# A gated attention and feed-forward block on one core: the order of the first batch's preparation is changed

## The chip, the core and the metric

The kernel runs on one core of a Trainium2 chip. The metric is the device time of one execution in microseconds (us), given as the median of the runs of the same program. The engines are PE (matrix products), DVE (the vector engine), ACT (the scalar engine), POOL (GpSimd) and SP, which only issues transfers. Each works through its own list of instructions in the order in which they are written, and they meet only at semaphores.

## The reference

For x of shape (8, 512, 256), in float32 (normalisation over the last axis, weights 256 x 256 and 1024 x 256):

```
xn = layernorm(x)
q, k, v = gelu(xn @ W1n + b1n) @ W2n + b2n            # n = q, k, v
scores  = tril(q @ k^T / sqrt(256 * 512))             # no softmax
s       = layernorm(scores @ v) * ln_w + ln_b
Wq1, Wq2 = clip(round(W / (mean(abs(W)) + eps)), -1, 1)   # ternary W1 and W2 of the FFN
g       = silu(relu(xn @ Wq1^T + b1) @ Wq2^T + b2)
out     = x + s * g
```

## The kernel before

Every engine's program is written out by hand. A batch (one of the eight 512 x 256 slices of x) goes through the stages below on PE; batch 0 is written apart (`first=True`), batches 1 to 6 run in a loop, batch 7 is apart again. Most operands are split in a rounded part ("hi") and the rest ("lo"), and a product is the sum of three products of such parts (`split_product`, line 843; all its matmuls show as L849 in the profile). Each hi part is made by ACT or POOL and each lo part mostly by DVE.

PE's stages in a batch are: layer one (six 128 x 512 products in the order `ORDER`, each followed on ACT by two GELU passes, L443 and L444, and on DVE by one `g_lo`, L653), K (two products that make z), V, F1 (eight products with the ternary W1), the key sum D, the scores S, Y0, Y1 (FFN output with the ternary W2), the weighted sums O, and Y2. Eight PSUM banks are handed round; `claim` waits until the bank's former content has been read.

Batch 0 has work that no other batch has:

- **Transposes.** DVE normalises the first batch (`x_normalise0`, L576), PE transposes it (`transpose_x`, L833), ACT and DVE make hi and lo parts (`xT_hi` at L427, `xT_lo` at L633).
- **Folding.** q and k are only needed as a product, so W2q and W2k are multiplied into one matrix: `fold_weights(0)` and `(1)` on PE, `fold_hi` on ACT (L431), `fold_lo` on DVE (L622, L624). The bias terms are `fold_z_bias` (twice) and `fold_d_bias`, each two matmuls of one column; DVE copies their results at L676 and L677.
- **Quantising.** ACT and DVE sum the absolute values of W1 (`abs_sum1`, L402; L637) and of W2 (`abs_sum2`, L408), PE adds over partitions (`sum_partitions`), DVE makes the thresholds (`thresholds`, L589, L591) and then the ternary weights: `quantise1(0)` and `(1)` for the two halves of W1 (L596 a comparison, L598 a comparison with subtraction), `quantise2` for five of the eight blocks of W2. POOL does the other three blocks (`quantise_rest`: L310, L311, L314). It begins when DVE has finished `quantise2` (semaphore `w2_quantized`). Y0 on PE waits for all of W2 (`w2_rest_quantized`) and for all eight `r_lo` parts of DVE (L743).
- **Parts of the key sum.** `e32` is made by DVE (L667, L678); in batch 0 POOL makes its parts (L339, L341).
- **Second batch's input.** `x_statistics(1)` on DVE (L554 to L547), then POOL normalises two tiles (`xn1_tile`, L303) and DVE two.

`v_shift_of` on ACT (L413) sums the rows of W2v, which POOL then needs for the centred W2v. PE begins with `WARM_UP` matmuls on a tile of ones (L840), whose result nobody reads.

SP issues the loads in one order: half of x[0], W1k, W2q, W1q, W2k, W2v, x[1], W1v, W1 of the FFN in two parts, W2 of the FFN. The biases (`cols`) and the other half of x[0] come from ACT's queue.

Of the kernel before, what the change touches and what calls it, by code (L numbers as in the profile page):

```python
# [27 lines left out]
AT_X0, AT_X1 = ((2, 3), (4, 6)), 30  # L28
# [6 lines left out]
WARM_UP = 17  # L35


def gated_block(nc, x, x_t, x_norm_rows, w_qkv, w1t, w2t, cols, rows, out):
# [13 lines left out]
    with ctx:  # L52
# [141 lines left out]
        def _(sp):  # L194
# [6 lines left out]
            sp.dma_start(x_all[:, 0, 0:2], x[0, 0:2 * P].rearrange("(t p) c -> p t c", p=P)).then_inc(x0_loaded[0], 16)  # L201
            load_square(1)
            sp.dma_start(w2q_raw[:, :, 0:C], w_qkv[3].rearrange("(k p) c -> p k c", p=P)).then_inc(qkv_loaded[3], 16)
            load_square(0)
            load_square(4)
# [49 lines left out]
        def _(pool):  # L255
# [72 lines left out]
            def batch(i, first=False, second_last=False, last=False):  # L328
                if first:
                    pool.wait_ge(x_rstd_made, 1)  # L330
                    pool.wait_ge(xT_summed, 2 * CK)
                    pool.wait_ge(w1_quantized, 1)
                    xn1_tile(0)
                    xn1_tile(1)
                    pool.wait_ge(v_shift_made, CK + 1)
                    nc.gpsimd.tensor_scalar(row[:, ROW_B2V], row[:, ROW_B2V], v_shift[:, CK:CK + 1], None,
                                            ALU.add).then_inc(v_centred, 1)
                    pool.wait_ge(e_made, 1)
                    nc.gpsimd.tensor_copy(e["hi"][:], e32[:]).then_inc(e_hi_made, 1)  # L339
                    pool.wait_ge(e_hi_made, 1)  # L340
                    nc.gpsimd.tensor_tensor(e["lo"][:], e32[:], e["hi"][:].bitcast(FP32),  # L341
                                            ALU.subtract).then_inc(e_split, 1)
                    pool.wait_ge(w2_quantized, 1)
                    quantise_rest()
                elif not last:
                    pool.wait_ge(xT_loaded, 16 * i)
                    pool.wait_ge(x_norm_loaded, 16 * i)
                    for k in range(CK):
                        xT_centre(k)
                        xT_scale(i + 1, k)  # L350
# [35 lines left out]
        def _(act):  # L386
# [48 lines left out]
            for k in range(CK):  # L435
                v_shift_of(k, raw_qkv[:, 5, k])

            def batch(i, first=False, last=False):
                for p, m in enumerate(ORDER):
                    act.wait_ge(l1_summed, 6 * i + p + 1)  # L440
                    b1 = col[:, COL_B1 + m:COL_B1 + m + 1]
                    pre = bank[(AT_L1 + p) % BANKS]
                    nc.scalar.activation(g["hi"][:, m], pre[:], ACT.Gelu, bias=b1)  # L443
                    nc.scalar.activation(pre[:], pre[:], ACT.Gelu, bias=b1).then_inc(l1_whole, 1)  # L444
                    if first and p < CK:
                        fold_hi(p)
                    if first and p == 0:
                        abs_sum1()
# [73 lines left out]
        def _(dve):  # L522
# [117 lines left out]
            def batch(i, first=False, second_last=False, last=False):  # L640
# [23 lines left out]
                if first:  # L664
                    fold_lo(0)
                    dve.wait_ge(fold_read, CK)
# [5 lines left out]
                if first:  # L672
                    fold_lo(1)
                    dve.wait_ge(fold_read, 2 * CK)
                    dve.wait_ge(biases_folded, 1)
                    nc.vector.tensor_copy(z_bias[:], FOLD_Z)  # L676
                    nc.vector.tensor_copy(d_const[:], FOLD_D).then_inc(bias_read, 1)  # L677
# [3 lines left out]
                if not first:  # L681
                    finish(i - 1, 2, 2, 2)
                if first:
                    thresholds(0)
                    dve.wait_ge(thr_made, 2)
                    quantise1(0)
                g_lo(2)
                g_lo(3)
                g_lo(4)
                g_lo(5)  # L690
                if first:
                    dve.wait_ge(w1_quantized, 1)
                    quantise1(1)
                    dve.wait_ge(w1_quantized, 2)
# [15 lines left out]
                if first:  # L710
                    thresholds(1)
# [106 lines left out]
        def _(pe):  # L818
# [41 lines left out]
            def fold_z_bias(n):  # L860

                split_product(FOLD_Z[:, n:n + 1], [(w2qT[:, k, n * P:(n + 1) * P], b2k[:, k:k + 1])
                                                   for k in range(CK)])
# [19 lines left out]
            def batch(i, first=False, last=False):  # L883

                pe.wait_ge(xT_hi_made, 2 * i + CK + 2)
                for p, m in enumerate(ORDER):
                    if first and p == 1:
                        pe.wait_ge(qkv_loaded[4], 16)
                        pe.wait_ge(b2q_beside, 1)
                    if first and p == 1:  # L890
                        fold_weights(0)
                    if first and p == 2:
                        fold_weights(1)
# [9 lines left out]
                    if first and p == 3:  # L903
# [80 lines left out]

            transpose_x(xn_made, AT_X0[0], (0, 1))
            pe.wait_ge(qkv_loaded[3], 16)
            pe.wait_ge(cols_loaded, 16)
            fold_z_bias(0)
            transpose_x(xn_made, AT_X0[1], (2, 3))
            fold_z_bias(1)  # L990
            fold_d_bias()
# [36 lines left out]
```

## Time and profile before

| | us |
|---|---|
| median of 3 runs | 307.86 |
| lowest and highest | 307.18, 310.16 |
| the profiled execution | 307.08 |
| its span, first to last instruction | 305.3 |

| engine | busy, us | share of the span |
|---|---|---|
| PE (matmul) | 299.3 | 98% |
| PE (weight load) | 268.6 | 88% |
| DVE | 247.9 | 81% |
| ACT | 222.2 | 73% |
| POOL | 132.8 | 43% |

The granted clock of PE is 1.000 over the span. The time outside the span is 307.08 - 305.3 = 1.8 us. In the timeline a row merges instructions of one kind that follow each other: start, time from the start of the first to the end of the last, engine, line, what is written and read, how many, and in brackets how long the engine stood idle before and what released it. The ends of matmuls and of pipelined vector instructions reach over the start of the next one, so a stage's length is best read from start to start.

### The profile page before, as it was taken

The numbers are of one execution on the slowest core, as the hardware profiler recorded it, in microseconds if no ns is written. First come the engines' busy times: TensorE is split into PE (matmuls) and PEld (weight loads), VectorE is DVE, ScalarE is ACT, GpSimd is POOL, SyncE is SP. The second block draws the span as 40 slices with busy tenths as digits, with TensorE's granted clock in tenths as the row PEclk, the third lists the DMA queues.
The fourth block names the chain that finished last, engine by engine and source line by source line (L and its number), as shares of the span: only waits on it lengthen the run. The fifth ranks groups of instructions, "written<-read, shape, count | busy, mean of one in ns | idle before, by whom it ended". The sixth has DMA issues, their size and how long they took to land.

```text
span 305.3 us, 5721 instructions
## 1 busy us (share of the span) xinstructions
PE 299.3 (98%) x1852; PEld 268.6 (88%) x1852; DVE 247.9 (81%) x548; ACT 222.2 (73%) x428; POOL 132.8 (43%) x104
## 2 busy tenths in 40 slices
PE   8999999999999999999999999999999999999994
PEld 8878899889988899888997889888998889988893
DVE  4989898957999589975999669995799858696686
ACT  3696958966785957949489577868679594895862
POOL 3954835076060942439151670608515291404100
PEclk9999999999999999999999999999999999999999
DMA  7960044500006000240005100060001500020001
GB/s 236 374 217 1 1 140 137 182 26 0 3 2 206 0 0 0 65 141 0 0 0 145 62 0 0 1 204 2 0 0 39 168 0 0 0 71 2 0 2 69
DMA packets 15228, 19.06 MB, mean 62 GB/s; under 512 B 1776, under 2 KB 12528, under 8 KB 15216
## 3 DMA queue, kind: packets, MB, share of 16 engines
q1 hardware_dynamic: 14656, 18.51, 18.6%
q10 hardware_dynamic: 560, 0.40, 0.4%
q8 instruction: 6, 0.10, 0.2%
q14 instruction: 6, 0.05, 0.1%
HBM read 14.69 MB, written 4.22 MB: 62 GB/s over the span
## 4 chain that ended last, share of the span: by engine, by line
PE 87%; DVE 6%; DMA 3%; SPq 1%; ACT 1%; issue 1%; POOL 0%; DVEq 0%
PE bank L849 86%; DMA x_all<-in_w1t 3%; DVE g L653 1%; SPq L199 1%; DVE gw L767 1%; DVE gw L645 0%; DVE w1q L598 0%; DVE x_all L647 0%; PE bank L957 0%; DVE e L756 0%; PE bank L958 0%; ACT r_lo L402 0%; DVE s_lo L738 0%; DVE gw L796 0%; PE bank L833 0%
## 5 line engine op out<-in xcount | busy, mean ns | idle before, releaser
L743 DVE TENSOR_TENSOR r_lo<-bank,r_hi 128x512 fp32r<-128x512 f32 x64 | 44.0, 691 | 34.7 <-ACT bank L465 34.6
L464 ACT ACTIVATE r_hi<-bank,col 128x512 fp32r<-128x512 f32 x64 | 47.0, 734 | 24.3 <-PE bank L849 24.3
L361 POOL TENSOR_TENSOR o_rstd<-o_var,neg_half 128x2 f32<-128x2 f32 x16 | 11.2, 699 | 82.8 <-ACT o_var L495 82.8
L465 ACT ACTIVATE bank<-bank,col 128x512 f32<-128x512 f32 x64 | 45.4, 710 | 0.0
L320 POOL TENSOR_TENSOR y<-y,xn 128x512 f32<-128x512 f32 x12 | 19.8, 1648 | 55.6 <-DMA y<-in_x_t 55.6
L849 PE MATMUL bank<-xT_lo,w1q 128*128 128x512 f32 x128 | 39.5, 390 | 0.0
L849 PE MATMUL bank<-xT_hi,w1q 128*128 128x512 f32 x128 | 39.5, 390 | 0.0
L443 ACT ACTIVATE g<-bank,col 128x512 fp32r<-128x512 f32 x48 | 34.2, 713 | 1.3 <-PE bank L849 1.1
L849 PE MATMUL bank<-w2q,r_lo 128*128 128x256 f32 x256 | 34.6, 278 | 0.0
L849 PE MATMUL bank<-w2q,r_hi 128*128 128x256 f32 x256 | 34.3, 276 | 0.0
L444 ACT ACTIVATE bank<-bank,col 128x512 f32<-128x512 f32 x48 | 33.0, 688 | 0.0
L479 ACT CAST s_hi<-s 128x512 fp32r<-128x512 f32 (+3 forms) x32 | 14.8, 461 | 23.2 <-DVE s L731 17.8
L849 PEld LDWEIGHTS bank<-w2q,r_lo 128*128 128x128 f32 x256 | 31.6, 188 | 0.0
L849 PEld LDWEIGHTS bank<-w2q,r_hi 128*128 128x128 f32 x256 | 31.4, 188 | 0.0
L653 DVE TENSOR_TENSOR g<-bank,g 128x512 fp32r<-128x512 f32 x48 | 30.7, 681 | 0.0
L849 PE MATMUL bank<-xT_hi,w_hi 128*128 128x512 f32 x96 | 30.3, 396 | 0.0
L849 PE MATMUL bank<-xT_hi,w_lo 128*128 128x512 f32 x96 | 29.7, 390 | 0.0
L849 PE MATMUL bank<-xT_lo,w_hi 128*128 128x512 f32 x96 | 29.6, 389 | 0.0
L849 PEld LDWEIGHTS bank<-xT_hi,w1q 128*128 128x128 f32 x128 | 24.0, 188 | 5.1
L849 PEld LDWEIGHTS bank<-xT_lo,w1q 128*128 128x128 f32 x128 | 23.5, 188 | 4.4
L849 PE MATMUL bank<-g,z_hi 128*128 128x512 f32 (+2 forms) x96 | 22.0, 337 | 0.0
L849 PEld LDWEIGHTS bank<-xT_hi,w_lo 128*128 128x128 f32 x96 | 18.0, 188 | 3.8
(143 smaller groups left out, 684.8 us busy)
## 6 DMA issues: line engine op xcount, KB each, us to landing
out<-x_all SPq DMA_DIRECT2D x15, 256.0 KB, 3.1
x_all<-in_x SPq DMA_DIRECT2D x7, 512.0 KB, 3.6
xn<-x_norm_rows SPq DMA_DIRECT2D x6, 512.0 KB, 4.0
y<-in_x_t SPq DMA_DIRECT2D x6, 512.0 KB, 4.7
x_all<-in_w1t SPq DMA_DIRECT2D x2, 512.0 KB, 7.6
x_all<-in_w2t SPq DMA_DIRECT2D x1, 1024.0 KB, 10.2
row<-in_rows SPq DMA_DIRECT2D x1, 512.0 KB, 4.7
x_all<-in_x SPq DMA_DIRECT2D x1, 256.0 KB, 3.2
```

Source lines behind the costliest of these rows:

```text
L199: sp.dma_start(raw_qkv[:, n], w_qkv[n].rearrange("(k p) c -> p k c", p=P)).then_inc(qkv_loaded[n], 16)
L320: nc.gpsimd.tensor_tensor(half, half, x_mean_all, ALU.subtract).then_inc(xT_centred, 1)
L361: nc.gpsimd.tensor_tensor(o_rstd[:, half], o_var[:, half], neg_half[:, half], ALU.pow).then_inc(o_rstd_made, 1)
L443: nc.scalar.activation(g["hi"][:, m], pre[:], ACT.Gelu, bias=b1)
L444: nc.scalar.activation(pre[:], pre[:], ACT.Gelu, bias=b1).then_inc(l1_whole, 1)
L464: nc.scalar.activation(r["hi"][:, f], pre[:], ACT.Relu, bias=b1)
L465: nc.scalar.activation(pre[:], pre[:], ACT.Relu, bias=b1).then_inc(f1_whole, 1)
L479: nc.scalar.copy(s["hi"][:, at], s32[:, at]).then_inc(s_hi_made, 1)
L653: nc.vector.tensor_tensor(g["lo"][:, m], bank[(AT_L1 + p) % BANKS][:], g["hi"][:, m].bitcast(FP32), ALU.subtract).then_inc(g_split, 1)
L743: nc.vector.tensor_tensor(r["lo"][:, f], bank[(AT_F1 + f) % BANKS][:], r["hi"][:, f].bitcast(FP32), ALU.subtract).then_inc(r_split, 1)
L767: nc.vector.scalar_tensor_tensor(gw[:, t], bank[(AT_O + t) % BANKS][:, 0:C], o_rstd[:, t:t + 1], row[:, ROW_LNW], ALU.mult, ALU.mult).then ...
L849: last = nc.tensor.matmul(dst, a, b, start=(n == 0), stop=(n == len(pairs) - 1))
```

## The change

Batches 1 to 7 keep their code. In batch 0 and ahead of it:

- SP loads W2q and W2k directly after the first half of x[0]; W1k becomes the fourth transfer of its queue (it was the second) and W1q the fifth (it was the fourth).
- PE does 14 warm-up matmuls where it did 17. Then come the bias folds and `fold_weights(0)` ahead of the transposes, and `fold_weights(1)` behind them; layer one has no fold in it. The sum over partitions for W1 stands after the fifth product of layer one and no longer after the fourth. One bank of the transposes is another (`AT_X0`).
- ACT does `fold_hi(0)` ahead of the first GELU, `fold_hi(1)` after the first pair, `abs_sum1` after the second pair.
- DVE does `fold_lo(0)` and the two bias copies ahead of `x_statistics(1)`, `fold_lo(1)` behind it; all six `g_lo` come ahead of `quantise1(0)`; `thresholds(0)` stands after the fourth `g_lo`, `thresholds(1)` after `quantise1(1)`.
- POOL makes the parts of the key sum and shifts the bias row ahead of `xn1_tile`, behind a wait for all six `g_lo`.

```diff
-AT_X0, AT_X1 = ((2, 3), (4, 6)), 30
+AT_X0, AT_X1 = ((2, 3), (4, 1)), 30
-WARM_UP = 17
+WARM_UP = 14
@@ SP
             sp.dma_start(x_all[:, 0, 0:2], x[0, 0:2 * P].rearrange("(t p) c -> p t c", p=P)).then_inc(x0_loaded[0], 16)
+            sp.dma_start(w2q_raw[:, :, 0:C], w_qkv[3].rearrange("(k p) c -> p k c", p=P)).then_inc(qkv_loaded[3], 16)
+            load_square(4)
             load_square(1)
-            sp.dma_start(w2q_raw[:, :, 0:C], w_qkv[3].rearrange("(k p) c -> p k c", p=P)).then_inc(qkv_loaded[3], 16)
             load_square(0)
-            load_square(4)
@@ POOL, batch 0
                 if first:
+                    pool.wait_ge(g_split, 6)
+                    pool.wait_ge(e_made, 1)
+                    nc.gpsimd.tensor_copy(e["hi"][:], e32[:]).then_inc(e_hi_made, 1)
...
                     pool.wait_ge(w1_quantized, 1)
                     xn1_tile(0)
                     xn1_tile(1)
...
                     pool.wait_ge(w2_quantized, 1)
                     quantise_rest()
@@ ACT
             for k in range(CK):
                 v_shift_of(k, raw_qkv[:, 5, k])
+            fold_hi(0)
...
-                    if first and p < CK:
-                        fold_hi(p)
                     if first and p == 0:
+                        fold_hi(1)
+                    if first and p == 1:
                         abs_sum1()
@@ DVE
+            fold_lo(0)
+            dve.wait_ge(biases_folded, CK + 1)
+            nc.vector.tensor_copy(z_bias[:], FOLD_Z)
+            nc.vector.tensor_copy(d_const[:], FOLD_D).then_inc(bias_read, 1)
             x_statistics(1, second=True)
+            fold_lo(1)
...
+                g_lo(2)
+                g_lo(3)
                 if first:
                     thresholds(0)
+                g_lo(4)
+                g_lo(5)
+                if first:
                     dve.wait_ge(thr_made, 2)
                     quantise1(0)
-                g_lo(2)
-                g_lo(3)
-                g_lo(4)
-                g_lo(5)
-                if first:
                     dve.wait_ge(w1_quantized, 1)
                     quantise1(1)
+                    thresholds(1)
@@ PE, layer one of batch 0
-                    if first and p == 1:
-                        fold_weights(0)
-                    if first and p == 2:
-                        fold_weights(1)
...
-                    if first and p == 3:
+                    if first and p == 4:
                         pe.wait_ge(abs1_summed[0], 1)
@@ PE, ahead of batch 0
-            transpose_x(xn_made, AT_X0[0], (0, 1))
-            pe.wait_ge(qkv_loaded[3], 16)
-            pe.wait_ge(cols_loaded, 16)
-            fold_z_bias(0)
-            transpose_x(xn_made, AT_X0[1], (2, 3))
-            fold_z_bias(1)
-            fold_d_bias()
+            pe.wait_ge(cols_loaded, 16)
+            fold_d_bias()
+            pe.wait_ge(qkv_loaded[3], 16)
+            fold_z_bias(0)
+            fold_z_bias(1)
+            pe.wait_ge(qkv_loaded[4], 16)
+            pe.wait_ge(b2q_beside, 1)
+            fold_weights(0)
+            transpose_x(xn_made, AT_X0[0], (0, 1))
+            transpose_x(xn_made, AT_X0[1], (2, 3))
+            fold_weights(1)
```

PE, from the bias folds or transposes to the end of the first product of layer one, before the change (`bank<-w2q_raw,raw_qkv` is `fold_weights`, `bank<-ident,xn` a transpose, the products of one column are the bias folds):

```order
L849 MATMUL bank<-col,w2q_raw 128x1 x2
L849 MATMUL bank<-col 128x1 x2
L849 MATMUL bank<-xT_hi,w_hi 128x512 [waits w_split,xT_hi_made]
L849 MATMUL bank<-xT_hi,w_hi 128x512
L849 MATMUL bank<-xT_hi,w_lo 128x512 x2
L849 MATMUL bank<-xT_lo,w_hi 128x512 [waits xT_split]
L849 MATMUL bank<-xT_lo,w_hi 128x512
L849 MATMUL bank<-w2q_raw,raw_qkv 128x257 [waits b2q_beside,qkv_loaded4]
L849 MATMUL bank<-w2q_raw,raw_qkv 128x257
L849 MATMUL bank<-xT_hi,w_hi 128x512 x2
```

The same place in the changed kernel, from the last warm-up matmuls on:

```order
L842 MATMUL bank<-ones 128x128 x13
L851 MATMUL bank<-col 128x1 [waits cols_loaded,consts_made]
L851 MATMUL bank<-col 128x1
L851 MATMUL bank<-col,w2q_raw 128x1 [waits qkv_loaded3]
L851 MATMUL bank<-col,w2q_raw 128x1 x3
L851 MATMUL bank<-w2q_raw,raw_qkv 128x257 [waits b2q_beside,qkv_loaded4]
L851 MATMUL bank<-w2q_raw,raw_qkv 128x257
L835 MATMUL bank<-ident,xn 128x128 [waits xn_made]
```

The folds stood inside layer one and behind the transposes; now three bias folds and the first weight fold stand ahead of the transposes.

DVE, from the lo parts of the transposed input to the first product's `g_lo`, before:

```order
L633 TENSOR_TENSOR xT_lo<-bank,xT_hi 128x256 [waits xT_hi_made] x4
L554 BN_STATS x_stats<-x_all 128x6 [waits x_loaded]
L554 BN_STATS x_stats<-x_all 128x6 x3
L544 BN_AGGR x_norm<-x_stats 128x2 [waits x1_stats_made]
L544 BN_AGGR x_norm<-x_stats 128x2 x3
L547 TENSOR_SCALAR x_var<-x_norm 128x4 [waits x1_stats_made]
L637 TENSOR_REDUCE abs_sum<-x_all 128x1 [waits raw1_loaded0]
L622 TENSOR_TENSOR w_lo<-bank,w_hi 128x256 [waits fold_hi_made,l1_whole]
L624 COPY d_weight<-bank 128x1
L667 TENSOR_SCALAR e<-bank,d_weight 128x512 [waits fold_read]
L653 TENSOR_TENSOR g<-bank,g 128x512 [waits l1_whole]
```

and now:

```order
L635 TENSOR_TENSOR xT_lo<-bank,xT_hi 128x256 [waits xT_hi_made] x4
L624 TENSOR_TENSOR w_lo<-bank,w_hi 128x256 [waits fold_hi_made]
L626 COPY d_weight<-bank 128x1
L639 COPY z_bias<-bank 128x2 [waits biases_folded]
L640 COPY d_const<-bank 128x1
L556 BN_STATS x_stats<-x_all 128x6 [waits x_loaded]
L556 BN_STATS x_stats<-x_all 128x6 x3
L546 BN_AGGR x_norm<-x_stats 128x2 [waits x1_stats_made]
```

The first `fold_lo` (L624 of the changed kernel), which waits for `fold_hi(0)` on ACT, now stands ahead of the statistics of the second batch.

POOL, in batch 0, as a difference (`L310` is the start of `quantise_rest`):

```order
 L299 TENSOR_TENSOR w2v_lo<-raw_qkv,w2v_hi 128x512 [waits w2v_hi_made]
-L303 TENSOR_SCALAR xn<-x_all,x_norm 128x256 [waits xT_summed,w1_quantized,x_rstd_made,rows_loaded]
+L332 CAST e_hi<-e 128x512 [waits e_made,g_split,rows_loaded]
+L334 TENSOR_TENSOR e_lo<-e,e_hi 128x512 [waits e_hi_made]
+L337 TENSOR_SCALAR row<-row,small 128x256 [waits v_shift_made]
+L303 TENSOR_SCALAR xn<-x_all,x_norm 128x256 [waits w1_quantized,xT_summed,x_rstd_made]
 L303 TENSOR_SCALAR xn<-x_all,x_norm 128x256
```

The two tiles of the second batch move behind the parts of the key sum; `quantise_rest` keeps its place and its wait.

## Rows read from the trace of the kernel before

**Rows 1.** The page: the span, and its part 4, the chain that ended last.

```profile
span 305.3 us, 5721 instructions
...
PE 87%; DVE 6%; DMA 3%; SPq 1%; ACT 1%; issue 1%; POOL 0%; DVEq 0%
```

**Rows 2.** The timeline of PE: start, length, engine, line, operation, count, idle before.

```profile
6.90 0.67 PE L833 MATMUL bank<-ident,xn 128*128 128x128 f32 x4
...
8.40 0.51 PE L849 MATMUL bank<-col,w2q_raw 128*128 128x1 f32 x4
8.77 0.59 PE L849 MATMUL bank<-col 128*128 128x1 f32 x4
9.21 0.70 PE L849 MATMUL bank<-xT_hi,w_hi 128*128 128x512 f32 x2
...
10.70 1.03 PE L849 MATMUL bank<-w2q_raw,raw_qkv 128*128 128x257 f32 x4
...
16.95 0.71 PE L849 MATMUL bank<-xT_hi,w_hi 128*128 128x512 f32 x2
...
19.80 0.62 PE L849 MATMUL bank<-g,w_hi 128*128 128x512 f32 x2
...
23.00 0.74 PE L849 MATMUL bank<-w2v_hi,g 128*128 128x256 f32 x4 [0.32 <-DVE g L653]
...
37.46 1.09 PE L849 MATMUL bank<-w2q,r_lo 128*128 128x256 f32 x8
```

**Rows 3.** Timeline of POOL: key-sum parts and its share of quantising W2.

```profile
25.75 1.29 POOL L341 TENSOR_TENSOR e_lo<-e,e_hi 128x512 fp32r<-128x512 f32 x1
30.63 2.22 POOL L310 TENSOR_SCALAR gw<-x_all,neg_thr 128x768 f32<-128x768 f32 x1 [3.59 <-DVE w2q L598]
...
35.20 1.85 POOL L314 TENSOR_TENSOR w2q<-w2q,gw 128x768 fp32r<-128x768 f32 x1
```

**Rows 4.** Timeline of DVE between 10 and 31 us.

```profile
10.28 1.41 DVE L554 BATCH_NORM_STATS2 x_stats<-x_all 128x6 f32<-128x256 f32 x4 [0.27 <-DMA x_all<-in_x]
...
16.30 0.42 DVE L622 TENSOR_TENSOR w_lo<-bank,w_hi 128x256 fp32r<-128x256 f32 x1 [1.01 <-ACT w_hi L431]
...
18.47 0.76 DVE L596 TENSOR_SCALAR s<-x_all,neg_thr 128x1024 f32<-128x1024 f32 x1
...
20.46 2.48 DVE L653 TENSOR_TENSOR g<-bank,g 128x512 fp32r<-128x512 f32 x4
22.86 0.88 DVE L596 TENSOR_SCALAR s<-x_all,neg_thr 128x1024 f32<-128x1024 f32 x1
...
25.23 1.41 DVE L699 SCALAR_TENSOR_TENSOR z_lo<-bank,z_bias,z_hi 128x512 fp32r<-128x512 f32 x2
...
30.56 0.69 DVE L743 TENSOR_TENSOR r_lo<-bank,r_hi 128x512 fp32r<-128x512 f32 x1
```

**Rows 5.** Warm-up matmuls (L840) by half microseconds: window, PE busy (instructions touched).

```profile
4.50:5.00 0.50, 0.50 (x4) 0.50 (x4) 1.00 0.87 284
...
5.50:6.00 0.50, 0.50 (x7) 0.50 (x7) 1.00 0.86 299
```

**Rows 6.** Timeline of SP, and DMA issues with us to landing (last column).

```profile
2.31 0.47 SPq L199 DMA_DIRECT2D raw_qkv<-in_W1q  x1
...
raw_qkv<-in_W1q SPq DMA_DIRECT2D x1, 256.0 KB, 4.9
```

**Rows 7.** Timeline of ACT ahead of and in layer one.

```profile
8.49 0.65 ACT L427 CAST xT_hi<-bank 128x256 fp32r<-128x256 f32 x2 [0.35 <-PE bank L833]
9.03 0.43 ACT L413 ACTIVATE o_square<-raw_qkv 128x256 f32<-128x256 f32 x1
...
10.90 0.69 ACT L443 ACTIVATE g<-bank,col 128x512 fp32r<-128x512 f32 x1 [0.95 <-PE bank L849]
...
12.05 0.39 ACT L431 CAST w_hi<-bank 128x256 fp32r<-128x256 f32 x1
...
13.59 1.06 ACT L402 ACTIVATE r_lo<-x_all 128x1024 fp32r<-128x1024 f32 x1 [1.15 <-DMA x_all<-in_w1t]
```

More of the change, by code:

```diff
@@ L329, in batch @@
                 if first:
+                    pool.wait_ge(g_split, 6)
+                    pool.wait_ge(e_made, 1)
+                    nc.gpsimd.tensor_copy(e["hi"][:], e32[:]).then_inc(e_hi_made, 1)
+                    pool.wait_ge(e_hi_made, 1)
+                    nc.gpsimd.tensor_tensor(e["lo"][:], e32[:], e["hi"][:].bitcast(FP32),
+                                            ALU.subtract).then_inc(e_split, 1)
+                    pool.wait_ge(v_shift_made, CK + 1)
+                    nc.gpsimd.tensor_scalar(row[:, ROW_B2V], row[:, ROW_B2V], v_shift[:, CK:CK + 1], None,
+                                            ALU.add).then_inc(v_centred, 1)
                     pool.wait_ge(x_rstd_made, 1)
@@ L334, in batch @@
                     xn1_tile(1)
[L335 to L342, printed above, removed]
                     pool.wait_ge(w2_quantized, 1)
@@ L664, in batch @@
                 if first:
-                    fold_lo(0)
                     dve.wait_ge(fold_read, CK)
@@ L672, in batch @@
                 if first:
-                    fold_lo(1)
                     dve.wait_ge(fold_read, 2 * CK)
-                    dve.wait_ge(biases_folded, 1)
-                    nc.vector.tensor_copy(z_bias[:], FOLD_Z)
-                    nc.vector.tensor_copy(d_const[:], FOLD_D).then_inc(bias_read, 1)
                 nc.vector.scalar_tensor_tensor(e32[:], bank[(AT_L1 + 1) % BANKS][:], d_weight[:, 1:2], e32[:],
@@ L682, in batch @@
                     finish(i - 1, 2, 2, 2)
+                g_lo(2)
+                g_lo(3)
                 if first:
                     thresholds(0)
-                    dve.wait_ge(thr_made, 2)
-                    quantise1(0)
-                g_lo(2)
-                g_lo(3)
                 g_lo(4)
@@ L691, in batch @@
                 if first:
+                    dve.wait_ge(thr_made, 2)
+                    quantise1(0)
                     dve.wait_ge(w1_quantized, 1)
                     quantise1(1)
+                    thresholds(1)
                     dve.wait_ge(w1_quantized, 2)
@@ L710, in batch @@
                 if first:
-                    thresholds(1)
                     dve.wait_ge(e_split, 1)
@@ L862, in fold_z_bias @@
                 split_product(FOLD_Z[:, n:n + 1], [(w2qT[:, k, n * P:(n + 1) * P], b2k[:, k:k + 1])
-                                                   for k in range(CK)])
+                                                   for k in range(CK)]).then_inc(biases_folded, 1)
             def fold_d_bias():
@@ L886, in batch @@
                 for p, m in enumerate(ORDER):
-                    if first and p == 1:
-                        pe.wait_ge(qkv_loaded[4], 16)
-                        pe.wait_ge(b2q_beside, 1)
-                    if first and p == 1:
-                        fold_weights(0)
-                    if first and p == 2:
-                        fold_weights(1)
                     if first and p % 2 == 0:
```

## Prediction, made before the changed kernel ran

> **What bounds the kernel now.** I read the page first. The chain that ended last is PE for 87% of a span of 305.3 us [rows 1], so the question is where PE, which works in program order, is held up. The timeline of PE shows only one stop inside the kernel: V of batch 0 starts at 23.00 after 0.32 us of waiting for the last `g_lo` on DVE. From there on PE runs without a gap, through Y0 of batch 0 at 37.46 and on to the end [rows 2]. The change touches batch 0 and what is ahead of it, nothing behind Y0 of batch 0. So the time of the profiled execution can be written as start of Y0 + 269.62: 305.3 - 37.46 = 267.84 behind it, and 1.78 around the span (307.08 - 305.3). Whatever moves that start moves the end by as much, if nothing later becomes late.
>
> Y0 waits for three things: PE's own queue, the eight `r_lo`, and the ternary W2. The last is nearly as late as PE: POOL begins its three blocks at 30.63, released by DVE's `quantise2`, and ends at 35.20 + 1.85 = 37.05 [rows 3]. From DVE's next start, 30.56 [rows 4], to that end is 6.49 us, and only 37.46 - 37.05 = 0.41 us are left to PE. So there is a second chain, DVE up to `quantise2`, then POOL, that ends 0.41 us ahead of PE. What idles on DVE in it is small: 0.27 us before 10.28 (its work before ended at 10.01) and 1.01 us before 16.30 [rows 4]. The reader is to see that a gain on PE alone is worth 0.41 us and no more; beyond that only what DVE gains counts.
>
> **PE's side.** Removed from the stretch of layer one: two `fold_weights`. From 10.70 to 16.95 PE does two folds, three products and one sum over partitions; the two products from 16.95 to 19.80 take 2.85, so three take 4.27, and the sum is like a bias fold of the same shape, 8.77 - 8.40 = 0.37 [rows 2]. 6.25 - 4.27 - 0.37 = 1.61, or 0.80 a fold.
>
> Three warm-up matmuls less: each is two records. Near 4.5 us four records are touched in half a microsecond, after 5.5 seven [rows 5], so the ones that fall away are of the fast kind, about 0.1 us a record, 0.6 us in all. The last column but two, the granted clock, says 1.00 in both rows, so it does not show this change of pace. The first transposes started at 6.90 [rows 2], right behind the warm-up; now it ends at about 6.3. Then three bias folds of 0.37 to 7.4, `fold_weights(0)` to 8.2, eight transposes (two groups of four, 0.5 each without the tail of the row's 0.67) to 9.2, `fold_weights(1)` to 10.0. ACT makes the second half's hi parts in 0.65 from shortly behind the transposes [rows 7]: 9.3 to 9.95. Layer one starts at about 10.0, against 9.21: 0.8 later. W2k must have landed by 7.4: it takes the third place in its queue, and even the transfer in the fourth landed at 2.31 + 4.9 = 7.2 [rows 6]. W1k now has that fourth place; its hi cast comes after 7.2, before ACT's next work at about 8.7, so it is hidden there. W1q is one place later, about 8 us, when POOL used it anyway.
>
> From layer one to V took 23.00 - 9.21 = 13.79 [rows 2]; less 1.61 for the folds and 0.32 for the wait it is 11.86. V could start at 21.9 and Y0 14.46 later (37.46 - 23.00), at 36.3. PE alone would gain 1.1 us.
>
> **ACT's side.** After 9.95 come the two `v_shift_of` of 0.43 and `fold_hi(0)` of 0.39 [rows 7], to 11.2. The first GELU starts 1.69 behind the start of layer one (10.90 - 9.21), at 11.7, and a pair takes 12.05 - 10.90 = 1.15: 12.85, `fold_hi(1)` to 13.2, second pair 14.4, `abs_sum1` 1.06 to 15.4 (W1 had landed at 13.59, so the wait of 1.15 for it goes), four pairs to 20.0. The sixth `g_lo` then needs DVE to be free.
>
> **DVE's side.** This is what decides.
> - Its xT_lo parts end 0.35 behind ACT's last hi part: 10.3, against 10.01: +0.3.
> - `fold_lo(0)` now waits for `fold_hi(0)`, which stands behind the `v_shift_of` on ACT: 10.3 to 11.2, +0.9. Queued behind it are the bias copies and all four statistics of x[1], which had their data. The waits of 0.27 and 1.01 are gone: -1.28, since `fold_hi(1)` at 13.2 comes before DVE is through the statistics (11.9 + 2.0).
> - The amount of work is the same, only reordered; the six `g_lo` end at about 20.8.
> - `quantise1(0)` ran with POOL idle, 18.47 to 20.46, 1.99. `quantise1(1)` ran beside POOL, 22.86 to 25.23, 2.37 [rows 4]. Now POOL is released by the sixth `g_lo` and works beside both halves: +0.38.
>
> Sum: 30.56 - 1.28 + 0.3 + 0.9 + 0.38 = 30.86. Plus POOL's 6.49: 37.35, and Y0 at 37.4, where PE has waited since 36.3. The eight `r_lo` at 0.6 each (20.46 to 22.86 for four) end at 35.7 and do not bind. So the start of Y0 moves by -0.06: nothing.
>
> **What lies beside other work at no cost.** POOL's key-sum parts and two tiles of x[1] come in another order; e_lo ended at 27.04 (25.75 + 1.29) and POOL then idled 3.59 us [rows 3], and now it starts them at 20.8, as before. If this cover were gone, POOL would start its W2 share late, one for one. `thresholds(1)` earlier on DVE: same two instructions. Behind Y0 DVE and ACT are 1 us further than before relative to PE, so nothing there is later.
>
> **Bounds of the unknown.** The extra wait for `fold_hi(0)` was never seen: nothing if the transposes come as early as before, 1.4 if they come 0.5 later than I think; I take 0.9, by the rows of ACT. The price of POOL's company: below, 0; above, one whole POOL instruction of 1.29 for each of the two instructions of `quantise1(0)`, 2.6; I take 0.38, from the same pair of instructions. The Trainium skill, SBUF — State Buffer, section "Who interferes with whom", says that VectorE and GpSimd share a port pair as an exclusive lock, so that the later one blocks for the whole instruction; by that the term would be 1.3 to 2.6. The rows show 0.38 for the second half under the same company, and that is what the sum uses.
>
> **Rivals.**
> 1. PE's arrival counts (0.2). DVE's chain is about 1.1 us shorter than I think: no company price (-0.38) and a wait for `fold_hi(0)` under 0.3 (-0.6). For it: all of DVE's old waits do go. Against it: the order on ACT. Y0 at 36.4: 307.08 - 1.1 = 306.0, as a median 306.7.
> 2. Slower: DVE and POOL hold each other up in `quantise1(0)` (0.15). The two instructions cost 1.3 to 2.6 more and not 0.38, so Y0 starts 0.9 to 2.2 later: median 308.7 to 310.0. It decides once `quantise1(0)` takes over 2.8 us. Against it is the 2.37 of the half that already had company [rows 4].
> 3. PE waits 1.1 us at Y0 and comes back at the lower of its two clock levels (0.03). Rows 5 give about half the pace there; four microseconds of it cost 2 to 4 us: 310 to 312. Against it: the wait of 0.32 left the pace as it was. The Trainium skill, TensorE: Matmul & The Clock Gate, part "The HAM clock gate", says that an idle PE falls back to 1.2 GHz; no row here shows how long it must be idle.
> 4. Faster by over 3 us (0.02): the folds, the wait and the start add up to less than that.
>
> **Numbers.** The forecast (0.6): the start of Y0 moves by -0.8 to +0.8. The profiled execution was 307.08 and the median of three runs 307.86, 0.78 above; I keep that distance: 307.0 by the profile, 307.8 as a median, 307.0 to 308.6 for this case alone. Towards rival 1 the range reaches 306.3, towards rival 2 309.2. About 1% is what a measurement of this kernel can tell from no change, 3.1 us. Only rival 4 is faster by that (0.02), part of rival 3 and the end of rival 2 slower (0.04), the rest is within 1% (0.94).
>
> **What would show it.** Right: PE starts layer one near 10.0, V near 21.9, and has a gap of about 1 us before Y0, released by POOL's last W2 instruction; DVE idles 0.9 before its first `fold_lo`, not at 16; `quantise1(0)` takes 2.4. Wrong: no gap before Y0 and a start near 36.3 (rival 1), `quantise1(0)` over 2.8 (rival 2), matmuls at half the pace behind a gap (rival 3), or a new wait behind Y0, which would break the step that everything later only shifts.

## The result, and the profile after

| | median, us | runs |
|---|---|---|
| before, on the same chip | 308.32 | 9 |
| changed | 311.43 (310.03 to 311.91) | 9 |

The ratio is 1.0087, with a 95% interval from 1.0072 to 1.0102: the change made the kernel slower by 2.2 to 3.1 us. The forecast was no change, 307.8, with a range up to 309.2. The profiled execution took 311.49, with this span and this chain that ended last (before: [rows 1]):

```profile
span 309.8 us, 5707 instructions
...
PE 81%; DVE 10%; issue 1%; ACT 1%; POOL 0%
```

PE is on the chain for 81% and no longer 87%, DVE for 10% where it was 6%. Where PE is held up shows in its timeline (columns as in rows 2):

```profile
7.25 0.51 PE L851 MATMUL bank<-col 128*128 128x1 f32 x4
...
11.24 0.73 PE L851 MATMUL bank<-xT_hi,w_hi 128*128 128x512 f32 x2
...
18.81 0.58 PE L851 MATMUL bank<-abs_sum,ones 128*128 128x1 f32 x4 [0.47 <-DVE g L660]
...
23.44 0.64 PE L851 MATMUL bank<-w2v_hi,g 128*128 128x256 f32 x4
...
38.23 0.33 PE L953 MATMUL bank<-g,z_hi 128*128 128x256 f32 x1
39.97 1.18 PE L851 MATMUL bank<-w2q,r_lo 128*128 128x256 f32 x8 [1.41 <-POOL w2q L314]
...
46.67 0.50 PE L851 MATMUL bank<-v_hi,s_hi 128*128 128x256 f32 x2 [0.35 <-DVE s_lo L740]
...
52.93 0.62 PE L851 MATMUL bank<-xT_hi,w_hi 128*128 128x512 f32 x2
```

Against [rows 2], layer one starts 2.03 us later (9.21), V 0.44 later (23.00), Y0 2.51 later (37.46). The last row is the start of batch 1. Before it stood here (with the first weighted sum):

```profile
42.92 0.28 PE L849 MATMUL bank<-v_hi,s_hi 128*128 128x256 f32 x1
...
49.09 0.69 PE L849 MATMUL bank<-xT_hi,w_hi 128*128 128x512 f32 x2
```

So batch 1 starts 3.84 us later: 2.51 up to Y0 and 1.33 between Y0 and batch 1, where I had forecast a mere shift. The rest of the 4.5 us between the two spans, 0.7, lies in the batches behind. From one layer one to the next a batch takes 35.8 to 36.0 us there, or 36.1 to 36.4. The profile of the kernel before has none of the longer kind, that of the changed kernel has two; but the kernels below have between none and four of them, and e11, the kernel before with one small edit, has two. So I count that as scatter; what makes a batch long stays open.

POOL, the changed kernel (to be held against [rows 3]):

```profile
14.58 1.29 POOL L293 TENSOR_TENSOR w_lo<-raw_qkv,w_hi 128x512 fp32r<-128x512 f32 x1
...
24.10 2.15 POOL L334 TENSOR_TENSOR e_lo<-e,e_hi 128x512 fp32r<-128x512 f32 x1
26.22 1.37 POOL L337 TENSOR_SCALAR row<-row,small 128x256 f32<-128x256 f32 x1
27.59 2.94 POOL L303 TENSOR_SCALAR xn<-x_all,x_norm 128x256 f32<-128x256 f32 x2
...
37.90 1.81 POOL L314 TENSOR_TENSOR w2q<-w2q,gw 128x768 fp32r<-128x768 f32 x1
39.67 2.43 POOL L357 TENSOR_TENSOR v_lo<-v,v_hi 128x1024 fp32r<-128x1024 f32 x1
```

DVE, the changed kernel (to be held against [rows 4]):

```profile
12.29 0.42 DVE L624 TENSOR_TENSOR w_lo<-bank,w_hi 128x256 fp32r<-128x256 f32 x1 [0.47 <-ACT w_hi L432]
...
14.67 1.22 DVE L549 TENSOR_SCALAR x_var<-x_norm 128x4 f32<-128x4 f32 x1
...
22.20 0.69 DVE L660 TENSOR_TENSOR g<-bank,g 128x512 fp32r<-128x512 f32 x1 [0.35 <-ACT bank L446]
22.80 0.74 DVE L598 TENSOR_SCALAR s<-x_all,neg_thr 128x1024 f32<-128x1024 f32 x1
23.58 1.51 DVE L600 SCALAR_TENSOR_TENSOR w1q<-x_all,thr,s 128x1024 fp32r<-128x1024 f32 x1
25.13 1.66 DVE L598 TENSOR_SCALAR s<-x_all,neg_thr 128x1024 f32<-128x1024 f32 x1
...
28.13 0.14 DVE L591 TENSOR_SCALAR thr<-bank 128x1 f32<-128x1 f32 x1
...
33.27 4.87 DVE L745 TENSOR_TENSOR r_lo<-bank,r_hi 128x512 fp32r<-128x512 f32 x8
38.06 4.20 DVE L753 TENSOR_SCALAR xn<-x_all,x_norm 128x256 f32<-128x256 f32 x2
```

and two of these groups in the kernel before, with POOL's `v_lo` there:

```profile
12.13 0.22 DVE L547 TENSOR_SCALAR x_var<-x_norm 128x4 f32<-128x4 f32 x1
...
37.18 0.73 DVE L751 TENSOR_SCALAR xn<-x_all,x_norm 128x256 f32<-128x256 f32 x2
...
37.58 2.59 POOL L356 TENSOR_TENSOR v_lo<-v,v_hi 128x1024 fp32r<-128x1024 f32 x1 [0.53 <-ACT v_hi L468]
```

The row of the two xn tiles, taken apart (shortest, median and longest in ns, first and last start in us):

```profile
L753 DVE TENSOR_SCALAR xn<-x_all,x_norm x2: 1806/2138/2471, 38.1 to 39.8; 128x256 f32<-128x256 f32 x2
```

The reader is to see operations that are long only because of their company. `x_var` works on four elements a partition, took 0.22 us and now takes 1.22: it ends at 15.89, and POOL's `w_lo` ends at 14.58 + 1.29 = 15.87. The second comparison of `quantise1` takes 1.66 instead of 0.88: it starts at 25.13, POOL's `e_lo` runs until 24.10 + 2.15 = 26.25, and the comparison ends at 26.79. It goes both ways: this `e_lo` took 1.29 in the kernel before [rows 3]. The two xn tiles take 4.20 instead of 0.73. The first starts at 38.06, takes 1.81 and ends at 39.87, just behind POOL's last W2 instruction (37.90 + 1.81 = 39.71). The second takes 2.47 and ends at 42.26, just behind POOL's `v_lo` (39.67 + 2.43 = 42.10). Before, they fell into a hole of POOL: its W2 share ended at 37.05 and `v_lo` waited 0.53 for ACT. Now `v_hi` is ready before POOL is through, POOL goes from one operation straight to the next, and each of the two tiles has to wait out one POOL instruction. DVE does get its turn where one POOL instruction gives way to the next, but its next tile meets the next POOL instruction. The Trainium skill, SBUF — State Buffer, section "Who interferes with whom", says just this: the ports that VectorE and GpSimd share are locked for a whole instruction. The ends of these rows agree with it.

### The profile page after: what moved, and what is told of

It is laid out like the page before. It is cut to its first block, busy times and chain, and to the rows that moved or that the text cites. A ratio compares the mean times of both kernels' runs of the same rounds, so it can differ in the third digit from the quotient of the medians.

```text
span 309.8 us, 5707 instructions
## 1 busy us (share of the span) xinstructions
PE 301.6 (97%) x1846; PEld 270.3 (87%) x1846; DVE 252.9 (82%) x548; ACT 222.2 (72%) x428; POOL 134.3 (43%) x104
## 4 chain that ended last, share of the span: by engine, by line
PE 81%; DVE 10%; issue 1%; ACT 1%; POOL 0%
PE bank L851 80%; DVE xn L753 1%; DVE s L598 1%; DVE e L758 1%; DVE s_lo L740 1%; DVE gw L769 1%; DVE s L733 1%; DVE w2q L600 1%; DVE w1q L600 1%; DVE gw L652 0%; DVE s L730 0%; DVE r_lo L745 0%; ACT s_hi L481 0%; DVE g L660 0%; DVE x_all L654 0%
## 5 line engine op out<-in xcount | busy, mean ns | idle before, releaser
L362 POOL TENSOR_TENSOR o_rstd<-o_var,neg_half 128x2 f32<-128x2 f32 x16 | 11.2, 701 | 84.7 <-ACT o_var L497 84.7
```

The lines of the kernel that those rows point to most:

```text
L362: nc.gpsimd.tensor_tensor(o_rstd[:, half], o_var[:, half], neg_half[:, half], ALU.pow).then_inc(o_rstd_made, 1)
```

## Experiments

Ratios are to the kernel before on the same chip, with their 95% interval. The columns in between are from one profiled execution each: start of layer one (L1), from there to Y0, and from Y0 to the start of batch 1. The differences take out what happens ahead of layer one. e1 to e4 ran on one chip, e5 to e8 on a second, e9 to e11 on a third and e12 on a fourth, each with the kernel before beside them but not the changed kernel, so a difference between ratios from two chips is less firm than one within a chip.

| kernel | L1 at | L1 to Y0 | Y0 to batch 1 | ratio |
|---|---|---|---|---|
| before | 9.21 | 28.25 | 11.63 | 1 |
| changed | 11.24 | 28.73 | 12.96 | 1.0087 (1.0072 to 1.0102) |
| e1_warm17 | 11.83 | 28.71 | 12.89 | 1.0111 (1.0097 to 1.0126) |
| e2_pool_old | 10.24 | 29.11 | 12.89 | 1.0111 (1.0091 to 1.0132) |
| e3_start_old | 9.06 | 29.78 | 12.89 | 1.0098 (1.0083 to 1.0113) |
| e4_start_only | 10.18 | 29.55 | 11.62 | 1.0073 (1.0060 to 1.0086) |
| e5_xn_late | 10.25 | 28.74 | 11.71 | 1.0069 (1.0053 to 1.0084) |
| e6_pool_free | 10.46 | 27.82 | 12.91 | 1.0071 (1.0050 to 1.0093) |
| e7_xvar_late | 10.26 | 28.06 | 12.85 | 1.0066 (1.0053 to 1.0079) |
| e8_all_three | 11.03 | 27.00 | 11.70 | 1.0008 (0.9997 to 1.0018) |
| e9_all_three_six | 10.19 | 25.88 | 11.63 | 0.9963 (0.9946 to 0.9981) |
| e10_old_start_six | 9.25 | 27.69 | 11.63 | 0.9983 (0.9971 to 0.9995) |
| e11_before_six | 9.39 | 27.74 | 11.63 | 0.9997 (0.9986 to 1.0008) |
| e12_warm10_six | 11.45 | 26.21 | 11.59 | 0.9973 (0.9941 to 1.0004) |

### Which part is slow: e1 to e4

**e1_warm17**, on the changed kernel:

```diff
-WARM_UP = 14
+WARM_UP = 17
```

> The changed kernel with 17 warm-up matmuls again; nothing else. Theory A (the shorter warm-up is why PE still runs at the slow pace at 7 us, where before it became fast near 5): the fast pace comes near 5 us, layer one starts near 10.0 instead of 11.24, and the median falls by 1 to 1.5 us, to about 310. Theory B (when the pace rises differs from execution to execution and has nothing to do with the three matmuls): layer one starts at 11 to 12 in an execution where it comes late, and the median is within 0.6 us of the changed kernel (311.4), rather above it.

Layer one started at 11.83, later still, and the ratio rose by 0.0024. Theory A falls. It was not for want of the three matmuls that the fast pace came late; with them back it came no sooner, and they only stand ahead of the folds. When the pace rises differs between executions: among the eight profiles of this start with 14 warm-up matmuls (the changed kernel, e2, e4 to e9) layer one starts at 10.2 to 10.5 in six and at 11.0 to 11.2 in two.

**e2_pool_old**, on the changed kernel: POOL's block of batch 0 in the order of before.

```diff
-                    pool.wait_ge(g_split, 6)
-                    pool.wait_ge(e_made, 1)
-                    nc.gpsimd.tensor_copy(e["hi"][:], e32[:]).then_inc(e_hi_made, 1)
...
-                    pool.wait_ge(v_shift_made, CK + 1)
...
                     xn1_tile(0)
                     xn1_tile(1)
+                    pool.wait_ge(v_shift_made, CK + 1)
...
+                    pool.wait_ge(e_made, 1)
+                    nc.gpsimd.tensor_copy(e["hi"][:], e32[:]).then_inc(e_hi_made, 1)
...
```

> The changed kernel with POOL's order of before (tiles of x[1] first, then bias row, then the key-sum parts). Theory C (DVE and POOL hold each other up in quantise1, which costs about 1 us): quantise1(0) takes 2.0 instead of 2.33 and quantise1(1) 2.4 instead of 3.0, and DVE reaches quantise2 about 1 us earlier; but e_split then comes at about 31.4 and quantise2 waits for it, so Y0 moves by -0.3 to +0.6 and the median stays at 311 to 312. If instead the order of POOL is what made the change slow by itself, the median falls back to about 309.

The timeline of DVE in this kernel:

```profile
21.79 0.75 DVE L597 TENSOR_SCALAR s<-x_all,neg_thr 128x1024 f32<-128x1024 f32 x1
...
23.89 0.75 DVE L597 TENSOR_SCALAR s<-x_all,neg_thr 128x1024 f32<-128x1024 f32 x1
...
26.06 0.15 DVE L590 TENSOR_SCALAR thr<-bank 128x1 f32<-128x1 f32 x1
...
30.13 0.89 DVE L597 TENSOR_SCALAR s<-x_all,neg_thr 128x1280 f32<-128x1280 f32 x1 [0.60 <-POOL e_lo L341]
```

The two halves take 2.10 and 2.17 us, where the changed kernel takes 2.33 and 3.00, so their company cost about 1.1 us. But DVE then stands still 0.65 us ahead of V's read and 0.60 ahead of `quantise2`, since POOL is late. One cost takes the other's place, as theory C said; POOL's order alone is not what made the change slow.

**e3_start_old**: the kernel before with the reordered DVE (all `g_lo` ahead of `quantise1(0)`, `thresholds(1)` behind `quantise1(1)`), the W1 sum after the fifth product, and POOL's new block. On the changed kernel, of which it takes back the start:

```diff
-AT_X0, AT_X1 = ((2, 3), (4, 1)), 30
+AT_X0, AT_X1 = ((2, 3), (4, 6)), 30
...
-WARM_UP = 14
+WARM_UP = 17
...
-            fold_lo(0)
-            dve.wait_ge(biases_folded, CK + 1)
...
+                    if first and p == 1:
+                        fold_weights(0)
+                    if first and p == 2:
+                        fold_weights(1)
```

> The kernel before with only the later parts of the change: g_lo ahead of quantise1, the earlier thresholds(1), the sum for W1 after the fifth product, POOL's new order. Loads, folds, warm-up (17) and the order on ACT are those of before. Theory D (the slow part is the new start: later layer one, statistics of x[1] beside POOL): the median is within 0.5 us of before (308.3). Theory E (the slow part is the new meeting of DVE and POOL: quantise1 beside POOL, then the two xn tiles of DVE blocked by POOL's v_lo): the xn tiles take 2 to 4 us instead of 0.73, and the median is 310 to 311.5.

The timeline of PE and DVE in this kernel:

```profile
9.06 0.70 PE L850 MATMUL bank<-xT_hi,w_hi 128*128 128x512 f32 x2
...
23.99 1.67 DVE L597 TENSOR_SCALAR s<-x_all,neg_thr 128x1024 f32<-128x1024 f32 x1
...
36.93 4.19 DVE L752 TENSOR_SCALAR xn<-x_all,x_norm 128x256 f32<-128x256 f32 x2
...
38.84 1.18 PE L850 MATMUL bank<-w2q,r_lo 128*128 128x256 f32 x8 [1.43 <-POOL w2q L314]
```

Layer one starts as in the kernel before, and still the ratio is 1.0098, as high as that of the whole change. Theory E holds and D falls as the main cause: the later start is not needed to lose 3 us.

**e4_start_only**: the changed kernel with DVE's `g_lo` and `quantise1`, the W1 sum and POOL in the order of before. On the kernel before, of which it changes the start alone:

```diff
-WARM_UP = 17
+WARM_UP = 14
...
+            fold_hi(0)
...
+            fold_lo(0)
+            dve.wait_ge(biases_folded, CK + 1)
...
-            fold_d_bias()
+            pe.wait_ge(qkv_loaded[4], 16)
+            pe.wait_ge(b2q_beside, 1)
+            fold_weights(0)
+            transpose_x(xn_made, AT_X0[0], (0, 1))
+            transpose_x(xn_made, AT_X0[1], (2, 3))
+            fold_weights(1)
```

> The changed kernel with only its start: loads, folds, 14 warm-up matmuls, fold_hi and fold_lo in the new places; g_lo and quantise1, the W1 sum and POOL in the order of before. Theory D: the median is 310 to 311.5, layer one starts at 10 to 11.3, x_var of x[1] takes about 1.2 us beside POOL. Theory E: the median is within 0.7 us of before (308.3), and the xn tiles of DVE take 0.7.

It is slower too, at 1.0073. The xn tiles take 0.73, as theory E says, and `x_var` takes 1.23, as theory D says. What comes on top is in neither theory. PE waits 1.83 us for `g_lo(0)` ahead of the W1 sum (which here follows the fourth product), since DVE now has the statistics of x[1] first; and then its clock is low. The timeline of PE in this kernel:

```profile
17.75 0.58 PE L850 MATMUL bank<-abs_sum,ones 128*128 128x1 f32 x4 [1.83 <-DVE g L659]
...
19.64 1.05 PE L850 MATMUL bank<-xT_lo,w_hi 128*128 128x512 f32 x2
```

and its windows of one microsecond (window, length, busy time of PE, weight load, DVE, ACT and POOL with their instructions, then the granted clock, DMA share and GB/s):

```profile
19.00:20.00 1.00, 1.00 (x3) 0.77 (x3) 0.94 (x2) 0.00 (x0) 0.00 (x0) 0.50 0.09 16
20.00:21.00 1.00, 1.00 (x4) 0.74 (x3) 1.00 (x1) 0.27 (x1) 0.00 (x0) 0.50 0.38 50
```

Two matmuls of 512 columns go 0.85 us apart instead of 0.46 (18.78, 19.64, 20.49): the granted clock is 0.50 of full speed, 1.2 GHz, from about 18.7 to 22. In e2, where the sum stands one product later, the wait is 0.43 and no such stretch follows. So moving the W1 sum behind the fifth product belongs to the new start. This is the mechanism of rival 3, in another place.

### The company of DVE and POOL, cause by cause: e5 to e8

**e5_xn_late**, on the changed kernel:

```diff
-                if first:
-                    dve.wait_ge(xn1_made, 2)
-                    for t in (2, 3):
-                        nc.vector.tensor_scalar(xn[:, t], x_all[:, 1, t], x_mean[:, t:t + 1], x_rstd[:, t:t + 1],
-                                                ALU.subtract, ALU.mult).then_inc(xn1_made, 1)
...
                 s_lo(TT - 1)
+                if first:
+                    dve.wait_ge(xn1_made, 2)
+                    for t in (2, 3):
...
```

> The changed kernel, with DVE's two xn tiles of x[1] moved behind the last s_lo, where POOL has nothing to do; nothing else. Theory C (in the changed kernel these two tiles took 4.20 us instead of 0.73, because POOL held the SBUF ports with its last W2 instruction and v_lo, and that made the scores late): the tiles take 0.7 to 0.8, the 0.35 us wait of the weighted sums for s_lo goes, Y0 starts where it did (about 40), and the time from Y0 to layer one of batch 1 falls from 12.96 to about 11.7, so the median falls by 0.8 to 1.3 us against the changed kernel. If that stretch keeps its length, the slow tiles were harmless.

The timeline of PE and DVE in this kernel:

```profile
38.99 1.17 PE L851 MATMUL bank<-w2q,r_lo 128*128 128x256 f32 x8 [1.42 <-POOL w2q L314]
...
43.78 0.73 DVE L764 TENSOR_SCALAR xn<-x_all,x_norm 128x256 f32<-128x256 f32 x2
...
50.70 0.68 PE L851 MATMUL bank<-xT_hi,w_hi 128*128 128x512 f32 x2
```

The tiles take 0.73, PE's wait for `s_lo` is gone, and Y0 to batch 1 is 11.71 (forecast 11.7) instead of 12.96. L1 to Y0 stays at 28.74. The median ratio falls by 0.0018, 0.55 us; the forecast was 0.8 to 1.3, and the intervals of the two ratios overlap, so in the median this is less firm than in the profile.

**e6_pool_free**, on the changed kernel:

```diff
-                    pool.wait_ge(g_split, 6)
                     pool.wait_ge(e_made, 1)
...
-                    pool.wait_ge(v_shift_made, CK + 1)
-                    nc.gpsimd.tensor_scalar(row[:, ROW_B2V], row[:, ROW_B2V], v_shift[:, CK:CK + 1], None,
-                                            ALU.add).then_inc(v_centred, 1)
...
-                    pool.wait_ge(w1_quantized, 1)
                     xn1_tile(0)
                     xn1_tile(1)
+                    pool.wait_ge(v_shift_made, CK + 1)
...
```

> The changed kernel, with POOL's e_hi and e_lo released by e_made alone and the xn tiles without their wait for W1, so that both run while DVE does g_lo (one operand in PSUM), not while it does quantise1. Theory C: quantise1(0) takes 2.0 to 2.1 and quantise1(1) 2.0 to 2.2 instead of 2.33 and 3.00, quantise2 and Y0 come 1.1 to 1.3 us earlier, the median falls by 1.0 to 1.3. Theory D (POOL's company in quantise1 is not the reason): no change of Y0, median as the changed kernel.

The timeline of DVE in this kernel:

```profile
22.03 0.95 DVE L596 TENSOR_SCALAR s<-x_all,neg_thr 128x1024 f32<-128x1024 f32 x1
...
24.33 0.85 DVE L596 TENSOR_SCALAR s<-x_all,neg_thr 128x1024 f32<-128x1024 f32 x1
...
26.42 0.15 DVE L589 TENSOR_SCALAR thr<-bank 128x1 f32<-128x1 f32 x1
```

2.30 and 2.09 us. The first half keeps some company, as the second xn tile ran into it; the second half lost its 0.9. L1 to Y0 falls by 0.91, the forecast was 1.1 to 1.3. In the median it is 0.5, where 1.0 to 1.3 was forecast.

**e7_xvar_late**, on the changed kernel: the one instruction that makes `x_var` of x[1] behind DVE's sum for W1.

```diff
-                    aggregate_tiles(range(TT), x1_stats_made, TT, x_var_made)
+                    aggregate_tiles(range(TT), x1_stats_made, TT, x_var_made, later=True)
...
+            nc.vector.tensor_scalar(x_var[:], x_rstd[:], EPS, None, ALU.add).then_inc(x_var_made, 1)
```

> The changed kernel, with the one small DVE operation x_var of x[1] (4 elements, 1.22 us beside POOL's w_lo, 0.22 before) moved behind the sum for W1. It then costs about 0.2 us. DVE has the first key-sum half and g_lo(0) 1.0 us earlier, PE's wait of 0.47 for g_lo ahead of the W1 sum goes, the last GELU comes 0.5 earlier. Theory C: Y0 0.5 to 0.9 earlier, median down by that. If DVE waits for ACT instead, Y0 moves by less than 0.2.

The timeline of DVE in this kernel:

```profile
15.22 0.16 DVE L648 TENSOR_SCALAR x_var<-x_norm 128x4 f32<-128x4 f32 x1
```

It takes 0.16, PE's wait for `g_lo` is gone, and L1 to Y0 falls by 0.67, within the 0.5 to 0.9 expected.

**e8_all_three**: the edits of e5, e6 and e7 together, and no other.

> The three edits of the runs beside it together on the changed kernel. Theory C: their gains add up to 2.3 to 3.3 us, so the median comes to 308 to 309 where the kernel before stands at 307.3 to 308.3; it does not pass the kernel before by more than 0.5 us, since layer one still starts 1 to 2 us later than before. If DVE and POOL holding each other up is not the reason, it stays over 310.

L1 to Y0 falls by 1.73 and Y0 to batch 1 by 1.26, about 3 us together; the single gains were 0.91 + 0.67 and 1.25, 2.8. The ratio falls from 1.0087 to 1.0008, 2.4 us, as theory C says. That these meetings of DVE and POOL account for the loss is shown: with them gone, so is the loss, with the new start still in place.

### What was left: e9 to e12

**e9_all_three_six**, on e8:

```diff
-        FQ = 5
+        FQ = 6
...
-                quantise(raw2[:, 0:FQ], w2q[:, 0:FQ], 1, flags.rearrange("p (f c) -> p f c", c=C),
-                         w2_quantized, 3)
+                flags2 = r["lo"][:, 4:7].rearrange("p a (f c) -> p (a f) c", c=C)
```

with the comparison's result of `quantise2` in a part of `r_lo` that is free then.

> The kernel with all three edits, and six of the eight blocks of W2 quantised by DVE (two by POOL; before five and three). DVE's quantise2 grows by about 0.4 us, POOL's share falls from 6.4 to about 4.5. Theory F (after the three edits Y0 is still held by POOL's share of W2, by 0.9 us): the wait ahead of Y0 is gone and Y0 starts 0.7 to 1.0 us earlier relative to layer one, the median falls by 0.7 to 1.2 us and passes the kernel before by 0.2 to 0.8 us. If Y0 then waits for r_lo instead, it gains less than 0.4.

The timeline of PE and POOL in this kernel:

```profile
10.19 0.74 PE L855 MATMUL bank<-xT_hi,w_hi 128*128 128x512 f32 x2
...
34.21 1.30 POOL L314 TENSOR_TENSOR w2q<-w2q,gw 128x512 fp32r<-128x512 f32 x1
...
36.07 1.09 PE L855 MATMUL bank<-w2q,r_lo 128*128 128x256 f32 x8
```

POOL is done at 35.51, PE comes to Y0 without a wait, at 36.07. L1 to Y0 falls by another 1.12, a little more than expected. The ratio is 0.9963 (0.9946 to 0.9981), 306.76 us against 308.03: this version beats both kernels, by 0.6 to 1.7 us against the one before.

**e10_old_start_six**: start of before, the reordered DVE and POOL of e6, xn tiles behind the scores, six blocks. It is e3 with the edits of e5 and e6 and this one (the comparison's result of `quantise2` goes where it goes in e9, here and in e11):

```diff
-        FQ = 5
+        FQ = 6
```

> The loads, folds, warm-up and ACT order of before; g_lo ahead of quantise1; POOL's key-sum parts and xn tiles beside g_lo; DVE's xn tiles behind the scores; six blocks of W2 on DVE. Theory G (the new start gains nothing, as the folds that it takes out of layer one come back as a later start of layer one): the same median as its neighbour with the new start, within 0.5 us. If the new start is a loss by itself, this is faster by 0.5 to 1 us; if a gain, slower by as much.

The ratio is 0.9983, 0.0020 above e9, or 0.6 us in favour of the new start; the intervals overlap by a little, so this is a lean and no proof. **e11_before_six**, the kernel before with six blocks:

```diff
-        FQ = 5
+        FQ = 6
```

> The kernel before, with six blocks of W2 on DVE and two on POOL and nothing else. PE reached Y0 of batch 0 at 37.46 with POOL done 0.41 us earlier, so POOL's share was not the bound: the median stays within 0.4 us of before. If it falls by more, PE's arrival was itself held back by the DVE and POOL chain.

0.9997 (0.9986 to 1.0008): nothing. POOL's share was not the bound of the kernel before.

**e12_warm10_six**, on e9:

```diff
-WARM_UP = 14
+WARM_UP = 10
```

> The version with the three edits and six blocks of W2 on DVE, with 10 warm-up matmuls instead of 14. Theory H (warm-up matmuls stand in the way of the folds wherever PE's pace rises late, 0.21 us a record): layer one starts 0.4 to 1 us earlier than the 10.2 to 11.2 seen with 14 of them, and since nothing but PE holds Y0 in this version, the ratio to the kernel before falls from 0.9963 to 0.993 to 0.995. Theory I (with fewer of them the folds and transposes only run at the slow pace instead, or wait for W2k): layer one starts at 10.0 to 11 and the ratio stays within 0.0015 of 0.9963.

The timeline of PE in this kernel:

```profile
5.46 0.58 PE L855 MATMUL bank<-col 128*128 128x1 f32 x4 [0.48 <-DMA col<-in_cols]
...
7.25 1.95 PE L855 MATMUL bank<-w2q_raw,raw_qkv 128*128 128x257 f32 x4 [0.32 <-DMA raw_qkv<-in_W2k]
```

and its windows of one microsecond (columns as in e4):

```profile
8.00:9.00 1.00, 1.00 (x4) 0.62 (x4) 0.38 (x1) 0.59 (x1) 0.19 (x1) 0.50 1.04 365
9.00:10.00 1.00, 1.00 (x6) 1.00 (x5) 0.32 (x1) 0.13 (x1) 0.92 (x2) 0.50 1.14 390
```

Here PE runs out of work twice, and the granted clock is 0.50 in the windows between 8 and 10: the first fold takes 1.74 (7.25 to 8.99) instead of 0.96 in the changed kernel. Layer one starts at 11.45 in this execution, later than either theory had it. The times spread from 305.12 to 309.55, where those of e9 lie between 306.09 and 308.75. The ratio is within 0.0015 of e9, as theory I says, but the best executions are better and the worst worse.

## Why the prediction was wrong, point by point

Two steps failed. The sum for DVE's chain put the start of `r_lo` at 30.86 and it was 33.27, mostly since DVE was held up by POOL in places where the sum had nothing; and "everything later only shifts" left out 1.33 us between Y0 and batch 1.

**Right: the second chain.** Y0 is held by DVE's `quantise2` and POOL's share of W2, and a gain on PE alone is worth almost nothing. PE waited 1.41 us at Y0 (forecast 1.1), released by POOL's last W2 instruction. That this comes so near is luck: PE's own work ahead of Y0 ended at 38.23 + 0.33 = 38.56, not 36.3, and POOL's share at 39.71, not 37.35, so both were about 2.3 us late. PE's own way was sized well for a kernel in which nothing else holds it: e9, which takes this wait away and those for `g_lo` and `r_lo` too, reaches Y0 at 36.07.

**Wrong by size: the start of layer one.** Forecast 10.0. It is 10.2 to 10.5 in six profiles of this start, 11.24 in the one of the changed kernel. [rows 5] showed the pace of one execution rising near 5 us, and I took that for a fixed time. In the changed kernel's profile it had not risen by 7, so the warm-up reached to 7.25 and not 6.3. A window of the warm-up matmuls there (columns as in [rows 5]):

```profile
6.50:7.00 0.50, 0.50 (x4) 0.50 (x4) 1.00 1.09 371
```

**Wrong: DVE's sum.** It gave 30.86 for the start of `r_lo`; it was 33.27. By terms, forecast and measured, start to start: end of the xT_lo parts +0.3 and +1.8 (11.82 against 10.01); the wait for `fold_hi(0)` 0.9 and 0.47; waits gone -1.28 and -1.28; `quantise1(0)` in company +0.38 and +0.34. Missing altogether, under "the amount of work is the same, only reordered": `x_var` +0.98 (14.67 to 15.81, was 0.16), the wait of 0.35 for the last GELU, and +0.63 for `quantise1(1)`, which takes 3.00 (25.13 to 28.13) where it took 2.37. Smaller gaps between instructions gave back 0.6. The term of `quantise1(1)` is the step "the rows show 0.38 for the second half under the same company": it was not the same company. The order of POOL's operations against DVE's was new, and how long one blocks the other depends on which of the two was first and how much of its instruction is left (the pair of DVE instructions takes between 1.99 and 3.00 us in the rows shown here).

**Wrong: the argument against the rule.** I set the rule of the exclusive lock that the Trainium skill has (SBUF — State Buffer, "Who interferes with whom") aside because one row showed 0.38. That row was one meeting, in which the parts that overlap happened to be small. Rival 2 had the right mechanism but the wrong place, and its mark, `quantise1(0)` over 2.8 us, was not reached (2.33). What POOL's company cost DVE ahead of `r_lo`, 0.34 + 0.98 + 0.63 = 1.95, lies in that rival's 1.3 to 2.6, but in three places, of which it had one.

**Wrong: "Behind Y0 DVE and ACT are 1 us further than before relative to PE, so nothing there is later".** Being further is what did the harm. `v_hi` was ready before POOL ended its W2 share at 39.71, POOL's hole of 0.53 us closed, and the xn tiles, harmless at 37.18, were blocked for 3.5 us. DVE's scores, and by them the weighted sums, became late; e5 shows it. The step "everything later only shifts" failed with it: 1.33 us.

By the ratio the change costs 2.7 us (3.1 between the two medians). Of this the three causes tried alone gave back 0.55 (e5), 0.5 (e6) and 0.65 us (e7), each with an interval about as wide as itself, and together 2.4 (e8).

## What to carry to other kernels

Where DVE and POOL both work from SBUF, cost every DVE operation of the kinds that were held up here (a tensor_scalar from SBUF, even of four elements), at up to the rest of the POOL instruction that is running, and the next one at the next POOL instruction. So write down what POOL does in each microsecond of the new order, not only how long its own chain is. A hole in which such an operation ran free before is a resource, and engines that become faster can close it. When a reordering shows no gain, look for the engine that now runs without a pause, and give DVE work with an operand in PSUM to do meanwhile: in e6 three `g_lo` took 1.87 us beside POOL's parts of the key sum, as they did in the changed kernel with POOL idle.

## What the runs showed of the hardware that I had not expected

- Each of two DVE tiles (0.73 us for both alone) waited out one of two POOL instructions that followed each other: 1.81 and 2.47 us in the changed kernel, 4.20 together, and 4.19 to 4.20 in e1, e2, e3 and e7 alike. In e6 DVE came 0.4 us later upon the first POOL instruction, and it took 3.76.
- The granted clock fell to 0.50 behind a wait of 1.83 us in e4, 0.9 us after PE was at work again, and between 8 and 10 us in e12, but not behind the wait of 1.41 us at Y0 in the changed kernel (1.00). What tells these cases apart was not tried. In the warm-up the pace doubles while the column says 1.00 throughout [rows 5].
- Behind the waits at Y0, the matmuls of 256 columns came 0.118 us apart (0.94 for eight) and not 0.113 (0.91) as in the kernel before, at a granted clock of 1.00. In the changed kernel, e3, e6 and e7 this lasted over all of Y0 and Y1, in e1, e2 and e8 only for some ten matmuls. The cause stays open.
